# Masked graph attention on 8192 nodes: the first eight row blocks computed in four column quarters, with partial sums kept in DRAM

## The chip, the cores and the metric

One of the cores of a Trainium2 chip runs the kernel. The metric is the device time of one execution in microseconds (us), as the median of several runs.

## What is computed

The reference, cut to its core (N = 8192, D = 256):

```python
h = jnp.maximum(_layernorm(x, axis=-1), 0.0)
h1 = h @ a[:D]; h2 = h @ a[D:]
e = jax.nn.leaky_relu(h1 + h2.T, negative_slope=0.01)
attention = jnp.where(adj > 0, e, NEG_BIG)
attention = jax.nn.softmax(attention, axis=1)
out = x + attention @ h
```

The 8192 x 8192 adjacency matrix is int32 (256 MB) and is read once. The exponential of a leaky ReLU is a maximum of two products: up to a factor that depends on the row alone and cancels in the softmax, the weight of row i and column j is max(r_i, g_j) * q_j * mask_ij. So r (one number for a row) and g and q (one each for a column) are made once, and q is multiplied into h.

## The kernel before

**Tiling.** The rows of adj are cut into 16 *blocks* of 512, the columns into 16 *chunks* of 512. A chunk is also 512 rows of h, which are four tiles of 128. The kernel goes block by block, and in each block through all chunks, two to a *step*: 16 x 8 = 128 steps. A step has four *pairs* k = 0 to 3, a pair being two tiles of h (256 columns of adj).

**One pair** goes through the engines so: SyncE loads a 1 MB piece of adj (one for a chunk) into adj_in; ScalarE turns it into a byte mask (convert); TensorE transposes the mask into PSUM (transpose_mask, tile T); VectorE makes W = max(r_rep, g) * T (weights, two instructions of 512); ScalarE rounds W to w_hi (round_w); VectorE makes the rest, w_lo = W - w_hi (subtract), two pairs later in its own order; TensorE does 24 matmuls (products): for each of four row tiles t and two tiles of h, w_hi with h_hi, w_hi with h_lo, w_lo with h_hi, into acc, four PSUM banks. h_hi has two more columns that sum the weights. w_lo has two buffers: subtract of pair g waits until TensorE has used pair g - 2.

**The end of a block.** ScalarE copies the four banks of acc to SBUF as soon as each is done (evacuate), in the first step of the next block; VectorE makes the reciprocals of the sums (denominators), ScalarE scales (normalise), GpSimd adds x (finish), ScalarE issues the store. The row of r for the next block is laid out over all partitions by TensorE (lay_out_r) and ScalarE (copy_r) into r_rep.

**The first block** also makes h, a chunk at a time, while it uses it: stats (VectorE, LayerNorm statistics), norm (GpSimd, the reciprocal root), h_rows (ScalarE, normalise and ReLU), scores (VectorE, two dot products with a for each of four tiles: eight instructions of 256), exps (ScalarE: r, g, q), round_h (ScalarE) and rest_h (GpSimd, scaled h and its rest h_lo), and TensorE sums h for rows without neighbours (sum_h).

Every engine runs its own instructions in the order in which the code issues them, the same function `iteration` for each; order between engines is by semaphores alone. The kernel's last block ends with 20 small VectorE instructions and four stores.

## Time and profile before

| | |
|---|---|
| median of 3 runs | 1688.58 us (1687.75 to 1688.63) |
| profiled execution, its own time | 1690.27 us |
| its span in the profile | 1688.5 us |
| TensorE, VectorE, ScalarE, GpSimd busy | 97%, 85%, 69%, 13% of the span |
| TensorE's mean granted clock | 0.993 of full |
| DMA | 294 MB, 174 GB/s |

Busy shares are averages over the whole span. What bounds a stage is read from that stage: how long it takes, and for whom its engines wait there. Matmuls are pipelined, so each lasts longer (280 ns) than the distance between two.

### The profile page before, as it was taken

How to read it: one execution, taken by the hardware profiler on the slowest of the kernel's cores; microseconds unless marked ns; L12 is line 12 of the kernel's file. 1: busy time of each engine (PE TensorE's matmuls, PEld its weight loads, DVE VectorE, ACT ScalarE, POOL GpSimd, SP SyncE). 2: the span in 40 equal slices, each digit the busy share in tenths (PEclk: the TensorE clock that was granted, in tenths of full speed). 3: DMA queues.
4: the chain of work that ended last, by engine and by line, in shares of the span. 5: the costliest groups of instructions: out<-in, count | busy, mean ns of one | idle time of the engine just before them, and what ended most of it. 6: DMA issues, size and time to landing. Idle time of an engine off the chain costs nothing.

```text
span 1688.5 us, 40886 instructions
## 1 busy us (share of the span) xinstructions
PE 1630.9 (97%) x13504; PEld 1621.2 (96%) x13504; DVE 1440.1 (85%) x2008; ACT 1164.5 (69%) x1158; POOL 220.4 (13%) x309
## 2 busy tenths in 40 slices
PE   4887999999999999999999999999999999999998
PEld 3777999999999999999999999999999999999998
DVE  6999888888888888888888888888888888888887
ACT  5777766767676666767677676766767676676764
POOL 4667301001010100101010010101001010100100
PEclk9999999999999999999999999999999999999999
DMA  6443455555555555555555555555555455555552
GB/s 199 146 147 112 164 173 182 191 166 185 171 198 174 165 191 167 197 174 187 175 172 186 174 199 168 180 174 185 187 173 184 167 196 174 172 192 167 192 173 88
DMA packets 142672, 294.08 MB, mean 174 GB/s; under 512 B 4928, under 2 KB 5440, under 8 KB 142656
## 3 DMA queue, kind: packets, MB, share of 16 engines
q1 hardware_dynamic: 138336, 278.15, 49.4%
q10 hardware_dynamic: 4320, 15.73, 2.5%
q8 instruction: 8, 0.13, 0.0%
q14 instruction: 8, 0.07, 0.0%
HBM read 285.47 MB, written 8.39 MB: 174 GB/s over the span
## 4 chain that ended last, share of the span: by engine, by line
PE 89%; DVE 8%; issue 2%; DMA 1%; DVEq 0%; ACT 0%; POOL 0%; SPq 0%; ACTq 0%
PE acc L609 28%; PE acc L612 27%; PE acc L611 27%; PE T L567 6%; DVE rep L460 3%; DVE w_lo L481 2%; DVE W L471 1%; DVE bst L442 1%; PE rep L582 0%; DMA r_rep<-in_L_gnn_a_dram 0%; DVE mv L447 0%; DMA xb<-in_x_dram 0%; ACT hb L307 0%; DVE adj_in L552 0%; DVE adj_in L547 0%
## 5 line engine op out<-in xcount | busy, mean ns | idle before, releaser
L609 PE MATMUL acc<-h_hi,w_hi 128*128 (+1 forms) x4096 | 1186.2, 290 | 28.9 <-DVE w_lo L481 28.9
L612 PE MATMUL acc<-h_hi,w_lo 128*128 (+1 forms) x4096 | 1159.2, 283 | 0.0
L611 PE MATMUL acc<-h_lo,w_hi 128*128 (+1 forms) x4096 | 1153.8, 282 | 0.0
L350 ACT ACTIVATE w_hi<-W 128x1024 fp32r<-128x1024 f32 x512 | 540.5, 1059 | 420.3 <-DVE W L471 367.0
L609 PEld LDWEIGHTS acc<-h_hi,w_hi 128*128 128x128 f32 x4096 | 776.3, 190 | 33.5 <-issue 33.1
L471 DVE SCALAR_TENSOR_TENSOR W<-r_rep,g_all,T 128x512 f32<-128x512 int8 (+1 forms) x1024 | 720.1, 745 | 103.3 <-DVE w_lo L481 90.5
L611 PEld LDWEIGHTS acc<-h_lo,w_hi 128*128 128x128 f32 x4096 | 781.1, 191 | 0.2
L612 PEld LDWEIGHTS acc<-h_hi,w_lo 128*128 128x128 f32 x4096 | 777.4, 190 | 0.0
L481 DVE SCALAR_TENSOR_TENSOR w_lo<-W,w_hi 128x1024 fp32r<-128x1024 f32 x512 | 627.7, 1226 | 123.4 <-PE acc L612 109.4
L341 ACT ACTIVATE mask<-adj_in,mhalf 128x2048 fp8e5<-128x2048 int32 x256 | 509.2, 1989 | 24.7 <-issue 23.2
L271 POOL TENSOR_TENSOR xb<-xb,stage 128x256 f32<-128x256 f32 x60 | 41.3, 689 | 1381.6 <-ACT hb L379 1361.3
L567 PE MATMUL T<-ident,mask 128*128 128x128 f32 x1024 | 154.7, 274 | 4.1 <-ACT mask L341 4.1
L567 PEld LDWEIGHTS T<-ident,mask 128*128 128x128 f32 x1024 | 119.4, 141 | 5.1 <-ACT mask L341 5.1
L273 POOL TENSOR_TENSOR xb<-xb,hb 128x256 f32<-128x256 f32 x60 | 58.6, 976 | 4.7
L250 POOL TENSOR_TENSOR h_lo<-hq,h_hi 128x1024 f32 (+1 forms) x16 | 45.8, 2861 | 6.7 <-POOL hq L244 4.3
L369 ACT ACTIVATE stage<-acc 128x258 f32<-128x258 f32 x60 | 23.3, 388 | 16.5 <-PE acc L612 16.4
L307 ACT ACTIVATE hb<-xb,shift,rstd 128x256 f32<-128x256 f32 x32 | 16.6, 590 | 25.5 <-POOL shift L233 21.7
L378 ACT ACTIVATE stage<-stage,rinv 128x256 f32<-128x256 f32 x60 | 29.7, 496 | 0.0
L379 ACT ACTIVATE hb<-hb,zrow 128x256 f32<-128x256 f32 x60 | 29.7, 495 | 0.0
L460 DVE SCALAR_TENSOR_TENSOR rep<-stage,r_rep 128x256 f32<-128x256 f32 x64 | 29.5, 530 | 0.0
L460 DVE SCALAR_TENSOR_TENSOR rep<-hb,r_rep 128x256 f32<-128x256 f32 x56 | 26.0, 533 | 0.0
L307 ACT ACTIVATE stage<-xo,shift,rstd 128x256 f32<-128x256 f32 x32 | 16.6, 590 | 12.7 <-POOL shift L233 12.7
(58 smaller groups left out, 277.5 us busy)
## 6 DMA issues: line engine op xcount, KB each, us to landing
adj_in<-in_adj_dram SPq DMA_DIRECT2D x256, 1024.0 KB, 5.2
xb<-in_x_dram ACTq DMA_DIRECT2D x15, 512.0 KB, 3.2
out_dram<-xb ACTq DMA_DIRECT2D x15, 512.0 KB, 2.6
xb<-in_x_dram SPq DMA_DIRECT2D x8, 512.0 KB, 3.3
xo<-in_x_dram SPq DMA_DIRECT2D x8, 512.0 KB, 3.3
adj_in<-in_x_dram SPq DMA_DIRECT2D x1, 512.0 KB, 3.2
out_dram<-adj_in SPq DMA_DIRECT2D x4, 128.0 KB, 1.9
r_rep<-in_L_gnn_a_dram SPq DMA_DIRECT2D x1, 256.0 KB, 6.0
```

The costliest lines, as they stand in the source:

```text
L250: nc.gpsimd.tensor_tensor(h_lo[:, tiles, 0:D], hq[:, :, :], h_hi[:, tiles, 0:D].bitcast(f32), ALU.subtract)
L271: nc.gpsimd.tensor_tensor(xb[:, t, :], xb[:, t, :], stage[:, t, 0:D], ALU.add).then_inc(s_fin, 1)
L273: nc.gpsimd.tensor_tensor(xb[:, t, :], xb[:, t, :], hshare, ALU.add).then_inc(s_o, 1)
L341: nc.scalar.activation(mask8[:, kc, :, :].rearrange("p t j -> p (t j)"), adj_in[:, kc, :, :].rearrange("p t j -> p (t j)"), ACT.Sign, bias ...
L350: nc.scalar.activation(w_hi[:, k % HL, :], W[:, k % 2, :], ACT.Relu).then_inc(s_hi, 1)
L460: nc.vector.scalar_tensor_tensor(out[:, j, :], h[:, e, :], 1.0, a_rep[:, j * D:(j + 1) * D], ALU.mult, ALU.mult, accum_out=h12[:, parity, ...
L471: last = nc.vector.scalar_tensor_tensor(W[:, k % 2, u * BLK:(u + 1) * BLK], r_rep[:, b % 2, :], g_all[:, ds(G * c + e, 1)], T8[:, k // 2, ...
L481: nc.vector.scalar_tensor_tensor(w_lo[:, k % LL, :], W[:, k % 2, :], 0.0, w_hi[:, k % HL, :].bitcast(f32), ALU.max, ALU.subtract).then_inc ...
L567: last = nc.tensor.transpose(T[:, kc, t * P:(t + 1) * P], mask_words[:, kc, t, :], ident[:])
L609: nc.tensor.matmul(acc[:, t, 0:WC], w_hi[:, k % HL, cols], rhs_hi, start=start and u == 0, stop=False)
L611: nc.tensor.matmul(acc[:, t, 0:D], w_hi[:, k % HL, cols], rhs_lo, start=False, stop=False)
L612: last = nc.tensor.matmul(acc[:, t, 0:WC], w_lo[:, k % LL, cols], rhs_hi, start=False, stop=stop and u == 1)
```

## The change

Steps are no longer numbered by block. They are grouped in *visits* of a block, described by a tuple V. Blocks 0 to 7 are visited four times, each time for a quarter of the columns (4 chunks, 2 steps); blocks 8 to 15 once, for all 16 chunks (8 steps). The order: the first quarter of blocks 0 to 7 (visits 0 to 7), the second (8 to 15), the third (16 to 23), and then in turn the last quarter of block m and the whole of block m + 8 (visits 24 to 39). There are 32 short visits and 8 long ones, again 128 steps.

Between its quarters, the sums of a block lie in DRAM (part_sums). Chunks 0 to 3 of h are made in visit 0, chunks 4 to 7 in visits 1 to 4 (phase "whole"), and chunks 8 to 15 over two visits each, 5 and 6 to 19 and 20 (phases "early" and "late"); their rounding (made=) comes in the visit after.

```diff
+                if V.full:
+                    steps(V, V.n0, 0, True, False)
+                    with eng.Fori(1, WIDE - 1) as it:
+                        steps(V, V.n0 + it, it * CI, False, False)
+                    steps(V, V.n0 + WIDE - 1, NB - CI, False, True)
+                else:
+                    steps(V, V.n0, V.c0, True, False)
+                    steps(V, V.n0 + 1, V.c0 + CI, False, True)
...
+            def quarter(v, q, prev, make=None, phase=None, made=None, nxt=None, head=False, turn=False):
+                visit(Visit(v=v, n0=2 * v, b=v - SH * q, c0=Q * q, full=False, prev=prev,
+                            pb=SH - 1 if turn else v - 1 - SH * q, f=None,
+                            pa=v - SH - 1, make=make, phase=phase, made=made,
+                            nxt=v + 1 - SH * q if nxt is None else nxt,
+                            head=head, tail=False))
+            def finals(m, prev):
+                n0 = 2 * NPART + (2 + WIDE) * m
+                visit(Visit(v=NPART + 2 * m, n0=n0, b=m, c0=NB - Q, full=False, prev=prev, pb=m + SH - 1, f=2 * m - 1,
+                            pa=2 * SH - 1, make=None, phase=None, made=None, nxt=m + SH,
+                            head=False, tail=False))
+                tail = isinstance(m, int) and m == SH - 1
+                visit(Visit(v=NPART + 2 * m + 1, n0=n0 + 2, b=m + SH, c0=0, full=True, prev="rest", pb=m, f=2 * m,
+                            pa=2 * SH + m, make=None, phase=None, made=None, nxt=None if tail else m + 1,
+                            head=False, tail=tail))
+            def two(j, q1, q2, prev1, prev2, nxt=None):
+                quarter(5 + 2 * j, q1, prev1, make=SH + j, phase="early", made=SH - 1 + j, nxt=nxt)
+                quarter(6 + 2 * j, q2, prev2, make=SH + j, phase="late", turn=q2 != q1)
+            quarter(0, 0, None, head=True)
+            quarter(1, 0, "first", make=Q, phase="whole")
+            with eng.Fori(2, 5) as v:
+                quarter(v, 0, "first", make=v + 3, phase="whole", made=v + 2)
+            two(0, 0, 0, "first", "first")
+            two(1, 0, 1, "first", "first", nxt=0)
+            with eng.Fori(2, 5) as j:
+                two(j, 1, 1, "added", "added")
+            two(5, 1, 2, "added", "added", nxt=0)
+            with eng.Fori(6, 8) as j:
+                two(j, 2, 2, "added", "added")
+            quarter(21, 2, "added", made=NB - 1)
+            if h_made is not None:
+                h_made()
+            quarter(22, 2, "added")
+            quarter(23, 2, "added", nxt=0)
+            if h_summed is not None:
+                h_summed()
+            finals(0, "added")
+            with eng.Fori(1, SH - 1) as m:
+                finals(m, "full")
+            finals(SH - 1, "full")
```

SyncE: x of a later chunk (load_more_x) and the row of r, which is now stored to DRAM and read back over all partitions (load_r), stand among the loads of adj. A partition now holds rows p, p + 128, p + 256, p + 384 of a block of adj and x, where it held rows 4p to 4p + 3 (`adj.rearrange("(b t p) j -> b p t j")` in place of `"(b p t) j"`).

```diff
-            def load_adj(b, it, kc, wait):
-                n = b * NI + it
+            def load_more_x(c):
+                sp.wait_ge(s_z, G * c)
+                sp.sem_inc(s_lgate, 1)
+                sp.dma_start(x_bufs[0], x_w[c]).then_inc(s_x[0], 16)
+            def load_adj(b, c, n, kc, wait):
                 if wait:
                     sp.wait_ge(s_mask, n * CI + kc - 1)
-                sp.dma_start(adj_in[:, kc, :, :], adj_v[b, :, :, ds((it * CI + kc) * BLK, BLK)]).then_inc(
...
+            def load_r(V):
+                if V.head:
+                    sp.wait_ge(s_aps, 1)
+                    sp.wait_ge(s_dot, 2 * G * Q + 2)
+                    sp.wait_ge(s_rd, 16 * 2)
+                else:
+                    sp.wait_ge(s_rd, 16 * (V.nxt + 1))
+                    sp.sem_inc(s_lgate, 1)
+                    sp.wait_ge(s_w, PI * V.n0)
+                    sp.sem_inc(s_lgate, 1)
+                    sp.wait_ge(s_rr, 16 * V.v)
+                sp.sem_inc(s_lgate, 1)
+                sp.dma_start(r_rep[:, (V.v + 1) % 2, :], r_dram[ds(V.nxt, 1), :].partition_broadcast(P)).then_inc(
+                    s_rr, 16)
+            def steps(V, n, c, first, last):
+                if V.head and first:
                     load_x(0, 0, False)
-                    sp.dma_start(a_rep, a_row.partition_broadcast(P)).then_inc(s_a, 16)
+                    sp.dma_start(r_rep[:, 1, :], a_row.partition_broadcast(P)).then_inc(s_a, 16)
                     load_x(1, 1, False)
                 for kc in range(CI):
-                    if first_block and not first:
-                        load_x(it * CI + kc, kc, True)
-                    load_adj(b, it, kc, not (first_block and first))
-                if last and first_block:
-                    sp.wait_ge(s_z, NB)
-                    sp.sem_inc(s_stored, 16)
-            run(sp, iteration)
+                    if V.head and not first:
+                        load_x(c + kc, kc, True)
+                    load_adj(V.b, c + kc, n, kc, not (V.head and first))
+                    if V.phase in ("early", "whole") and first and kc == 0:
+                        load_more_x(V.make)
+                    if V.nxt is not None and last and kc == (1 if V.head else 0):
+                        load_r(V)
```

GpSimd: from chunk 4 on it sums h itself (sum_rows), and adds the earlier quarters to a block's sums (add_prior).

```diff
+            def sum_rows(c):
+                for e in range(G):
+                    pool.wait_ge(s_hs, G * (c - Q) + e + 1)
+                    nc.gpsimd.tensor_tensor(hsum[:], hsum[:], hb[:, e, :], ALU.add).then_inc(s_hs, 1)
+            def rest_h(c, parity):
                 pool.wait_ge(s_hh, c + 1)
                 pool.wait_ge(s_hq, c + 1)
                 tiles = ds(G * c, G)
@@ -253,86 +345,105 @@
                                         q4[:, parity, :].rearrange("p (e o) -> p e o", o=1),
                                         h_hi[:, tiles, D:D + 1].bitcast(f32), ALU.subtract).then_inc(s_hl, 1)
...
-            def finish(b, t):
-                i = G * b + t
+            def add_prior(V):
+                pool.wait_ge(s_prior, 16 * (V.pa + 1))
+                pool.wait_ge(s_free, G * V.v)
+                nc.gpsimd.tensor_tensor(stage[:, :, :], stage[:, :, :], prior, ALU.add).then_inc(s_add, 1)
...
+                if V.head:
+                    for kc in range(CI):
+                        if c + kc + 2 < Q:
+                            norm(c + kc + 2, kc)
+                        if c + kc + 1 < Q:
+                            scale_h(c + kc + 1, (kc + 1) % CI)
+                            rest_h(c + kc + 1, (kc + 1) % CI)
+                if V.made is not None and first:
+                    scale_h(V.made, 0)
+                    sum_rows(V.made)
+                if V.prev in ("added", "rest") and first:
+                    add_prior(V)
+                if V.phase in ("early", "whole") and first:
+                    norm(V.make, 0)
+                if V.made is not None and first:
+                    rest_h(V.made, 0)
+                if V.prev in ("full", "rest") and last:
+                    for t in range(G):
+                        finish(V.f, t)
+            run(pool, steps)
```

ScalarE: the new stores and loads are issued from its queue, and the work on h is spread over the pairs k = 0 to 7 of a short visit.

```diff
+            def store_r(c):
+                act.wait_ge(s_ex, c + 1)
+                if not isinstance(c, int) or c > 0:
+                    act.wait_ge(s_rd, 16 * c)
+                act.dma_start(r_cols[c], r_all[:, ds(G * c, G)]).then_inc(s_rd, 16)
...
+            def evacuate(V):
+                if V.prev in ("first", "added"):
+                    if isinstance(V.v, int) and V.v == 1:
+                        act.wait_ge(s_hl, Q)
+                        act.wait_ge(s_hsum, Q)
+                    else:
+                        act.wait_ge(s_part, 16 * (V.v - 1))
+                elif isinstance(V.f, int) and V.f == 0:
+                    act.wait_ge(s_part, 16 * NPART)
+                else:
+                    act.wait_ge(s_o, G * V.f)
+                for t in range(G):
                     if t < G - 1:
-                        act.wait_ge(s_acc, (G - 1) * b + t + 1)
+                        act.wait_ge(s_acc, (G - 1) * (V.v - 1) + t + 1)
                     else:
-                        act.wait_ge(s_used, (b + 1) * PB)
-                    if t == 0:
-                        if not isinstance(b, int) or b > 0:
-                            act.wait_ge(s_o, G * b)
...
+            def store_part(V):
+                if V.prev == "first":
+                    act.wait_ge(s_free, G * V.v)
+                    act.dma_start(part[V.pb], stage[:, :, :]).then_inc(s_part, 16)
+                else:
+                    act.wait_ge(s_add, V.pa + 1)
+                    act.dma_start(part[V.pb], stage[:, :, :]).then_inc(s_part, 16)
+            def load_prior(V):
+                if isinstance(V.pa, int) and V.pa == 0:
+                    act.wait_ge(s_z, G * Q)
+                else:
+                    act.wait_ge(s_add, V.pa)
+                act.wait_ge(s_part, 16 * (V.pa + 1))
+                act.dma_start(prior, part[V.pb]).then_inc(s_prior, 16)
...
+            def side_work(V, k):
+                if V.made is not None:
+                    if k == 0:
+                        round_h(V.made, 0, [0, 1])
+                    if k == 2:
+                        round_h(V.made, 0, [2, 3])
+                        store_r(V.made)
+                if V.prev is not None:
+                    if k == 1:
+                        evacuate(V)
+                if V.phase == "whole":
+                    if k == 3:
+                        h_rows(V.make, 0, [0, 1])
+                    if k == 4:
+                        h_rows(V.make, 0, [2, 3])
+                if V.phase == "early":
+                    if k == 6:
+                        h_rows(V.make, 0, [0, 1])
+                    if k == 7:
+                        h_rows(V.make, 0, [2, 3])
+                if V.phase in ("whole", "late") and k == 7:
+                    exps(V.make, 0)
+                if V.prev in ("first", "added") and k == 4:
+                    store_part(V)
+                if V.prev in ("added", "rest") and k == 0:
+                    load_prior(V)
+                if V.prev in ("full", "rest"):
+                    if k == 2:
+                        load_x_again(V)
+                    if k == 4:
+                        normalise(V.f, 0)
+                    if k == 5:
+                        normalise(V.f, 1)
+                    if k == 6:
+                        normalise(V.f, 2)
+                        normalise(V.f, 3)
+                    if k == 7:
+                        store_out(V)
```

VectorE: scores now read a from PSUM (a_ps); statistics and scores are spread over the pairs of a visit.

```diff
+                    dve.wait_ge(s_z, G * c + e + 1)
                     for j in range(2):
                         dve.wait_ge(s_dot, 2 * G * c + 2 * e + j + 1)
-                        nc.vector.scalar_tensor_tensor(out[:, j, :], h[:, e, :], 1.0, a_rep[:, j * D:(j + 1) * D],
+                        nc.vector.scalar_tensor_tensor(out[j], h[:, e, :], 1.0, a_ps[:, j * D:(j + 1) * D],
                                                        ALU.mult, ALU.mult, accum_out=h12[:, parity, j, e:e + 1]
                                                        ).then_inc(s_dot, 1)
...
+            def side_work(V, k):
+                if V.phase == "whole":
+                    if k == 1:
+                        stats(V.make, 0, V.make - 1, [0, 1])
+                    if k == 2:
+                        stats(V.make, 0, V.make - 1, [2, 3])
+                    if k >= 4:
+                        scores(V.make, 0, [k - 4])
+                if V.phase == "early" and 1 <= k <= 4:
+                    stats(V.make, 0, V.make - 1, [k - 1])
+                if V.phase == "late" and k >= 4:
+                    if k == 4 and V.prev == "added":
+                        dve.wait_ge(s_add, V.pa + 1)
+                    scores(V.make, 0, [k - 4])
+                if V.prev in ("full", "rest") and k == 4:
+                    denominators(V)
```

**VectorE, where h is made.** Before, in the first block, all of a chunk's work on h (the statistics in tile mv, the eight scores in rep) stands between the weights of two pairs:

```order
L442 BN_STATS bst<-xo 128x6 x4
L447 BN_AGGR mv<-bst 128x2 x4
L481 SCALAR_TENSOR_TENSOR w_lo<-W,w_hi 128x1024
L471 SCALAR_TENSOR_TENSOR W<-r_rep,g_all,T 128x512 x2
L460 SCALAR_TENSOR_TENSOR rep,h<-hb,r_rep 128x256 x8
L481 SCALAR_TENSOR_TENSOR w_lo<-W,w_hi 128x1024
```

In the changed kernel, in visit 1 from its third pair on (the first half of the statistics stands just ahead), the same work is in pieces, one piece to a pair:

```order
L659 SCALAR_TENSOR_TENSOR w_lo<-W,w_hi 128x1024
L614 BN_STATS bst<-xb 128x6 x2
L620 BN_AGGR mv<-bst 128x2 x4
L649 SCALAR_TENSOR_TENSOR W<-r_rep,g_all,T 128x512 x2
L659 SCALAR_TENSOR_TENSOR w_lo<-W,w_hi 128x1024
L649 SCALAR_TENSOR_TENSOR W<-r_rep,g_all,T 128x512 x2
L659 SCALAR_TENSOR_TENSOR w_lo<-W,w_hi 128x1024
L638 SCALAR_TENSOR_TENSOR xo,h<-hb,a_ps 128x256 x2
L649 SCALAR_TENSOR_TENSOR W<-r_rep,g_all,T 128x512 x2
```

A pair of weights and its subtract now have at most a quarter of a chunk's scores or half its statistics beside them.

**GpSimd, the same chunks.** Before, in the loop over the first block's steps, it does the norm of one chunk and the scaled h (hq) and rest of the next:

```order
L226 TENSOR_TENSOR rstd<-mv,eps 128x4
L229 TENSOR_TENSOR nmean<-zeros,mv 128x4
L231 TENSOR_TENSOR rstd<-rstd,mhalf 128x4
L233 TENSOR_TENSOR shift<-nmean,rstd 128x4
L244 TENSOR_SCALAR hq<-stage,q 128x256 x4
L250 TENSOR_TENSOR h_lo<-hq,h_hi 128x1024
L252 TENSOR_TENSOR h_hi<-q,h_hi 128x4
```

Now, in visit 21 (the last one that finishes a chunk) and the four after it, hsum and the earlier sums (xo) are added as well; the visits 9, 11, ... 19 have the norm too, between the sum into stage and h_lo:

```order
L327 TENSOR_SCALAR hq<-hb,q 128x256 x4
L335 TENSOR_TENSOR hsum<-hsum,hb 128x256 x4
L352 TENSOR_TENSOR stage<-stage,xo 128x1032
L342 TENSOR_TENSOR h_lo<-hq,h_hi 128x1024
L344 TENSOR_TENSOR h_hi<-q,h_hi 128x4
L352 TENSOR_TENSOR stage<-stage,xo 128x1032 x4
```

Four instructions of 256 and one of 1032 elements a partition stand between the exponentials and the rest of h (h_lo).

**SyncE, the start.** Now, in visit 0 and the first step of visit 1, the row of r (r_rows) stands ahead of the fifth piece of adj:

```order
L231 DMA xb<-in_x_dram 128x1024
L243 DMA adj_in<-in_adj_dram 128x4x512
L231 DMA xo<-in_x_dram 128x4x256
L243 DMA adj_in<-in_adj_dram 128x4x512
L258 DMA r_rep<-r_rows 128x512
L243 DMA adj_in<-in_adj_dram 128x4x512
L237 DMA xb<-in_x_dram 128x1024
```

Before, the fifth piece followed the load of x alone, with no load of r anywhere in the queue.

## Rows read from the trace of the kernel before

**Rows 1.** Busy time by stretch: stretch, length, engines (instructions), granted clock, DMA, GB/s.

```profile
32.10:195.30 163.20, 133.88 (x933) 126.68 (x932) 152.63 (x416) 125.57 (x220) 105.97 (x142) 0.94 0.42 140
195.30:1681.30 1486.00, 1486.00 (x12539) 1486.00 (x12538) 1263.97 (x1502) 1022.32 (x909) 101.61 (x133) 1.00 0.53 178
1681.30:1688.50 7.20, 0.32 (x3) 0.12 (x1) 4.50 (x19) 0.00 (x0) 0.00 (x0) 0.76 0.21 73
```

**Rows 2.** The same view, one block of the steady part.

```profile
294.10:393.20 99.10, 99.10 (x839) 99.10 (x838) 84.49 (x101) 68.60 (x61) 6.79 (x9) 1.00 0.54 180
```

**Rows 3.** Waits, whole span: who waited for whom, us in total, times, longest.

```profile
PE acc L609 <- DVE w_lo L481: 28.9, 14, 2.8
```

**Rows 4.** Timeline of VectorE, one chunk of the first block: start, duration.

```profile
71.62 1.41 DVE L471 SCALAR_TENSOR_TENSOR W<-r_rep,g_all,T 128x512 f32<-128x512 f32 x2 [0.22 <-DVE w_lo L481]
72.94 1.40 DVE L442 BATCH_NORM_STATS2 bst<-xo 128x6 f32<-128x256 f32 x4
...
74.80 1.20 DVE L481 SCALAR_TENSOR_TENSOR w_lo<-W,w_hi 128x1024 fp32r<-128x1024 f32 x1
76.24 1.41 DVE L471 SCALAR_TENSOR_TENSOR W<-r_rep,g_all,T 128x512 f32<-128x512 f32 x2 [0.24 <-DVE w_lo L481]
77.56 0.79 DVE L460 SCALAR_TENSOR_TENSOR rep<-hb,r_rep 128x256 f32<-128x256 f32 x1
...
80.94 1.22 DVE L481 SCALAR_TENSOR_TENSOR w_lo<-W,w_hi 128x1024 fp32r<-128x1024 f32 x1
82.38 0.75 DVE L471 SCALAR_TENSOR_TENSOR W<-r_rep,g_all,T 128x512 f32<-128x512 f32 x1 [0.22 <-DVE w_lo L481]
```

**Rows 5.** Timeline of VectorE, three instructions that wait for nobody.

```profile
189.42 1.40 DVE L471 SCALAR_TENSOR_TENSOR W<-r_rep,g_all,T 128x512 f32<-128x512 int8 x2 [0.28 <-DVE w_lo L481]
190.74 1.22 DVE L481 SCALAR_TENSOR_TENSOR w_lo<-W,w_hi 128x1024 fp32r<-128x1024 f32 x1
192.06 1.41 DVE L471 SCALAR_TENSOR_TENSOR W<-r_rep,g_all,T 128x512 f32<-128x512 int8 x2
```

**Rows 6.** Timeline of GpSimd: two rests of h, one scaled h, one sum of 256.

```profile
33.10 2.22 POOL L250 TENSOR_TENSOR h_lo<-hq,h_hi 128x1024 fp32r<-128x1024 f32 x1
72.93 1.84 POOL L244 TENSOR_SCALAR hq<-stage,q 128x256 f32<-128x256 f32 x4 [3.00 <-ACT q L321]
75.11 2.94 POOL L250 TENSOR_TENSOR h_lo<-hq,h_hi 128x1024 f32 x1 [0.34 <-POOL hq L244]
576.07 0.64 POOL L271 TENSOR_TENSOR xb<-xb,stage 128x256 f32<-128x256 f32 x1 [75.55 <-ACT hb L379]
```

**Rows 7.** Timeline of VectorE beside the first row of rows 6.

```profile
33.16 2.45 DVE L460 SCALAR_TENSOR_TENSOR rep<-hb,r_rep 128x256 f32<-128x256 f32 x1
35.53 0.46 DVE L460 SCALAR_TENSOR_TENSOR rep<-hb,r_rep 128x256 f32<-128x256 f32 x1
```

**Rows 8.** Timeline of ScalarE at a block's end: first and last of four evacuations.

```profile
590.94 0.39 ACT L369 ACTIVATE stage<-acc 128x258 f32<-128x258 f32 x1 [0.21 <-PE acc L612]
...
593.00 0.39 ACT L369 ACTIVATE stage<-acc 128x258 f32<-128x258 f32 x1 [0.33 <-PE acc L612]
```

**Rows 9.** DMA issues of the page: count, KB each, median us to landing.

```profile
adj_in<-in_adj_dram SPq DMA_DIRECT2D x256, 1024.0 KB, 5.2
xb<-in_x_dram ACTq DMA_DIRECT2D x15, 512.0 KB, 3.2
```

**Rows 10.** Landing time of the first piece of adj alone, issued at 2.1 us.

```profile
DMA to landing us min/median/max: 9.1/9.1/9.1
```

**Rows 11.** Timelines at the start: ScalarE's first mask, VectorE's first weights, TensorE's first product.

```profile
17.52 1.99 ACT L341 ACTIVATE mask<-adj_in,mhalf 128x2048 fp8e5<-128x2048 int32 x1
21.86 1.38 DVE L471 SCALAR_TENSOR_TENSOR W<-r_rep,g_all,T 128x512 f32<-128x512 f32 x2
32.12 0.47 PE L609 MATMUL acc<-h_hi,w_hi 128*128 128x258 f32 x1
```

**Rows 12.** Group by line: GpSimd's reciprocal root, count, us busy, mean ns.

```profile
L231 POOL TENSOR_TENSOR rstd<-rstd,mhalf 128x4 f32<-128x4 f32 x16 | 19.5, 1217 | 0.0
```

## What I predicted before the run

> **What bounds the kernel now.** I first cut the span into stretches [rows 1]. From 195.3 to 1681.3 us TensorE is busy without a gap at full clock, while VectorE works 85% of the time: this part is TensorE's. A block takes 99.10 us there [rows 2], in about 836 matmuls, four of which lay out r; without them it is 98.6, or **12.33 us for a step** and 3.08 for a pair. From 32.1 to 195.3 us VectorE is busy 152.6 of 163.2 us and TensorE 82%, at a granted clock of 0.94: this stretch is VectorE's. It does the first block, 8 steps, for which TensorE would need 98.6. In the whole trace TensorE waits for w_lo at only 14 places, 28.9 us in all [rows 3]; the rest of its loss lies in stretched work and in the order of its queue. After the last product 7.2 us follow, which the change leaves alone.
>
> So the floor with VectorE out of the way is a start, 128 x 12.33, and 7.2. Before, the first product begins at 32.12 [rows 11], and 32.1 + 1578.2 + 7.2 = 1617.5; 15 blocks lose another 7 to the lay-outs, and the first block 64. These two sum to the span of 1688.5 and are all that the change can win, except for an earlier start. What VectorE does to a chunk is in [rows 4]: from the weights at 71.62 to those at 82.38 pass 10.76 us, of which 1.86 are statistics (72.94 to 74.80) and 3.38 scores (77.56 to 80.94), the rest two pairs. A pair that waits for nobody takes 2.64 us [rows 5], up to 2.76 with the write that the weights wait for [rows 4]; I take **2.7**. Against 3.08, VectorE has 0.38 us to spare in a pair and 3.1 in a short visit. Making one chunk costs it about 5.
>
> **The start, visit 0.** I followed the new order from semaphore to semaphore with the durations of [rows 4], [rows 6] and [rows 11]. ScalarE now converts the first mask ahead of h_rows; its data land at 2.1 + 9.1 = 11.2 us [rows 10], so h_rows starts at 13.2 where it could have at 11.6. But scores now follow tile by tile, and end at 17 as before. The mask was 1.99 us between exps and the copy of r [rows 11]; that is gone, and VectorE's first weights start at 19.9 in place of 21.86. The subtract stands right behind, and TensorE starts at about 27 in place of 32.1. From there on each chunk is a chain: ScalarE h_rows, exps, round_h and two roundings, GpSimd norm and rest, VectorE the rest. I get weights of pairs 2, 4 and 6 at 31.4, 42.6 and 52.9 us, no faster than the 10.76 of [rows 4]. Then SyncE: the load of r stands ahead of the fifth piece of adj and waits for the last scores (51.5). So that piece lands at about 57.7 (5.2 to 5.8 after its issue, [rows 9]), while ScalarE stands in its convert since 54.5 and, behind that, roundings of pairs 6 and 7; TensorE waits with pair 5 behind the transposes. A one-time stall of 3 us. **TensorE begins visit 1 at 71 us.** 126 steps remain: 71 + 1553 + 7 = **1631**. Bounds: 65 with the stall hidden, 75 with every wait a little longer.
>
> **Visits 1 to 4**, a whole chunk each. VectorE needs 8 x 2.7 + 1.9 + 3.1 = 26.6 against 24.7: +2 for visit 1. In visits 2 to 4 a wait is added: h_rows of the next chunk, at k = 3 on ScalarE, waits for the rest of the chunk before (s_hl), whose GpSimd work now stands behind four additions of 256 and the norm. By rows: scaled h 1.84 [rows 6], additions 4 x 0.64 to 0.9, norm some 2.3 with its root of 1.2 [rows 12], but h_lo can't start before round_h at k = 2, about 11 us after the exps; with its 2.2 to 2.9 [rows 6] s_hl comes at 14. Behind h_rows on ScalarE stands the convert of k = 4, and VectorE's scores wait for the tile. From exps to exps: 14 + 0.6 + 12.5 (four pairs with scores) + 1.9 = 29 against 24.7, so **+4.5 three times, 13.5** (from 2 each, with the wait hidden, to 6).
>
> **Visits 5 to 20**, half a chunk each. Statistics: 21.6 + 1.9 = 23.5; scores: 21.6 + 3.1 = 24.7. By themselves both fit. What doesn't is GpSimd. At 33.10 it starts h_lo, and VectorE's score of 33.16 lasts 2.45 in place of 0.46, until GpSimd is done at 35.3 [rows 6, 7]. At 75.11 it is the other way round: h_lo lasts 2.94, because VectorE's subtract runs until 76.0 [rows 4, 6]. So instructions with two SBUF inputs keep each other out; weights read T from PSUM and ran on beside it. The subtract is such an instruction, and so are h_lo, the 0.64 us sums [rows 6] and the new add_prior of 1032 elements, which I price as h_lo, 2.2. If it begins during a subtract it runs on for 2.2 us over weights of 1.3 and delays the next subtract by 0.8; if it begins during weights, by up to 2.2. I take 1.15 for each long one, 0.1 for a short one, 0.3 for the norm. Visits 9 to 20 are six couples: early 23.5 + 2 x 1.15 + 0.4 + 0.3 = 26.5 (+1.8), late 24.7 + 1.15 = 25.8 (+1.1), **6 x 2.9 = 17**. Visits 5 to 8 have no add_prior: +1. Bounds: 0, as VectorE has slack in other pairs and is one or two pairs ahead, to 2.2 for each long one, 35.
> The Trainium skill (SBUF — State Buffer, "SBUF: two separate sides") says that the pair of ports that VectorE and GpSimd share is an exclusive lock, held for the whole instruction, and that the second one blocks fully. By that rule read as 2.2 us for every long instruction the term would be 35; the one row with VectorE second shows it (2.45), the others only 0.3 (0.79 at 77.56).
>
> **Ends of visits.** 39 in place of 15. At a block's end ScalarE spends 2.5 us on evacuation, since it follows TensorE bank by bank (590.94 to 593.4 [rows 8]), and yet blocks take 99.10 without a gap. The stores and loads of sums (0.5 MB, priced as x, 3.2 us to landing [rows 9]) have from k = 4 to the next k = 1. DMA was at 0.53 of its time [rows 1] and gains a quarter in short visits: hidden. The row of r comes a step early: hidden. ScalarE works 8.5 us a step [rows 2], 17 in a short visit, plus 4 for h, 2.5 and up to three issues: near 24.7, no more. Denominators and finish lie in slack as before. For all this and for half-clock stretches while TensorE isn't full, 3 (0 to 20). Removed lay-outs are in the 12.33.
>
> **Sum.** 1631 + 2 + 13.5 + 1 + 17 + 3 = 1667.5, a span 21 shorter. The profiled run's own time was 1.8 over its span and 1.7 over the median; the difference of spans applied to the median, 1688.6 - 21, gives **1668 us**.
>
> **Rivals.**
> *VectorE and GpSimd don't hurt each other* in visits 5 to 20 (for: scores now read PSUM, and only 0.3 us was lost per chunk before): 1667.5 - 17 - 3 = 1648. Chance 0.2.
> *Ends of visits cost TensorE*, the other side: ScalarE's evacuation stands ahead of the convert and of round_w of k = 2, and behind it now come round_h, h_rows and DMA issues. If of each of the 24 new ends 1.2 us is exposed, it takes 29 and the kernel is slower, at 1697; it decides from 0.75 each (18 us). All 2.5 exposed would give 1728. For: ScalarE near 24 of 24.7. Against: none of 15 ends shows a gap. 0.15.
> *Adj comes slower.* Consecutive 2 KB pieces of a partition now lie 128 rows x 32 KB = 4 MB apart, before 32 KB. If that doubled the 5.2 us of a piece [rows 9], two would take 20.8 against 12.33 a step, some 2670 us; up to 6 us a piece it is hidden. No row shows such a stride, and the 512 rows read are the same. 0.02.
> The Trainium skill (DMA: Bandwidth & Descriptors, "Latency and other measured facts") reports half the rate for a row pitch of 4 MiB from partition to partition; that pitch here shrinks.
> *The quarters win nothing*: visit 0's chain and the waits of visits 1 to 4 repeat through visit 20, 4.5 each: 1631 + 90 - 30 for what overlaps, near 1688. 0.08.
> The forecast has 0.55, its own range 1658 to 1680.
>
> **Range and chances.** 1647 to 1690 takes in the first rival, the forecast and the last; outside are some 0.15 to 0.2. A change within 0.2%, 3.4 us, can't be told from none here. Faster 0.78 (0.55, 0.2, a little of the last), within 0.06, slower 0.16.
>
> **What would show it.** TensorE's first product at 27 us and visit 1's at 71; ScalarE waiting for the fifth adj piece; visits 2 to 4 at 29 us; couples 9 to 20 at 52 in place of 49.3; subtracts of over 1.3 us beside GpSimd's long additions; full blocks at 98.6. Wrong would make it: couples at 49.3 (first rival), or TensorE waiting at ends of visits 21 to 24, where no h is made (second).

## The result: 1671.3 us, 1.0% faster, and the profile after

The changed kernel takes **1671.31 us** (median of 4 runs, 1669.16 to 1673.48) against 1688.61 of the kernel before beside it: ratio 0.9897, 95% interval 0.9882 to 0.9913. I had forecast 1668, so the direction and the size hold. The terms of my sum do not all hold. Two of them are wrong and cancel, and that is luck.

The page of the changed kernel, its first lines and two groups:

```profile
span 1668.8 us, 39111 instructions
...
PE 1604.5 (96%) x13350; PEld 1594.2 (96%) x13350; DVE 1439.5 (86%) x2008; ACT 1184.9 (71%) x1240; POOL 359.2 (22%) x367
...
L659 DVE SCALAR_TENSOR_TENSOR w_lo<-W,w_hi 128x1024 fp32r<-128x1024 f32 x512 | 657.5, 1284 | 136.4 <-ACT w_hi L461 65.0
...
L352 POOL TENSOR_TENSOR stage<-stage,xo 128x1032 f32<-128x1032 f32 x24 | 75.6, 3148 | 212.7 <-ACT stage L480 212.6
```

GpSimd's addition of prior sums (L352) takes 3.15 us on the mean, while the subtraction (L659) that my forecast had it hold up is hardly longer than one alone, 1.28 against 1.22. In the waits, whole span, these three are of interest beside [rows 3]:

```profile
ACT stage L515 <- POOL xb L362: 40.3, 22, 2.7
PE T L769 <- ACT mask L452: 37.5, 13, 13.3
...
PE acc L807 <- DVE w_lo L659: 4.7, 4, 1.4
```

TensorE's 28.9 us of waits for w_lo are down to 4.7. It waits 37.5 us for masks from ScalarE, 25.5 of them before 60 us, at the start. Behind 770 us its transposes wait 14 times for 1.0 to 1.9 us, 22.3 us in all; the profile puts part of these down to the masks and part to VectorE's W. ScalarE in turn waits 40.3 us for GpSimd (L515 is the division of a finished tile, L362 GpSimd's last addition to a tile). By stretch, in the columns of [rows 1], these are the start to visit 1, visit 1, visits 2 to 4, 5 to 25, 26 to the last product, and the tail:

```profile
25.60:70.60 45.00, 33.30 (x225) 32.14 (x225) 30.77 (x78) 28.42 (x48) 15.95 (x22) 0.85 0.44 134
70.60:96.50 25.90, 25.49 (x209) 24.83 (x208) 24.45 (x48) 20.29 (x27) 7.79 (x11) 1.00 0.64 200
96.50:180.30 83.80, 78.33 (x626) 75.05 (x626) 79.64 (x146) 64.01 (x86) 36.54 (x43) 1.00 0.62 199
180.30:773.80 593.50, 592.51 (x4995) 592.24 (x4994) 540.82 (x771) 447.21 (x480) 163.91 (x141) 1.00 0.72 220
773.80:1661.60 887.80, 866.48 (x7272) 863.80 (x7271) 746.42 (x896) 611.42 (x581) 123.42 (x119) 1.00 0.61 186
1661.60:1668.80 7.20, 0.50 (x5) 0.29 (x3) 4.66 (x19) 0.00 (x0) 0.00 (x0) 0.88 0.22 73
```

In 180.3 to 773.8 us, where I had put 17 us of loss, TensorE stands still for 1 us. From 773.8 us on, where the final visits are, it stands still for 21.3 us.

For a finer account I took the start of TensorE's first product of each visit from the trace and subtracted 12.33 us for each of its steps. What is left is the visit's loss:

| part | forecast | measured |
|---|---|---|
| first product starts | 27 | 25.6 |
| visit 1 starts | 71 | 70.6 |
| loss of visit 1 | 2 | 1.3 |
| of visits 2 to 4 | 13.5 | 9.7 (3.3, 3.3, 3.2) |
| of visits 5 to 8 | 1 | 0 |
| of visits 9 to 20 | 17 | 0.1 |
| of visits 21 to 38 (ends and clock) | 3 | 27.5 (0.4 before visit 25) |

From visit 26 on each quarter loses 2.0 us and each whole visit some 1.7; one whole visit, 27, loses 3.6. The quarters lose it in one pair, k = 6, which takes 5.2 us.

**How a final visit loses 2 us.** ScalarE at the end of visit 26 (start, duration), after the third tile, which it normalises from 788.83 us on:

```profile
791.97 0.51 ACT L515 ACTIVATE stage<-stage,rinv 128x256 f32<-128x256 f32 x1 [2.25 <-POOL xb L362]
792.39 0.49 ACT L516 ACTIVATE hb<-hb,zrow 128x256 f32<-128x256 f32 x1
792.79 1.04 ACT L461 ACTIVATE w_hi<-W 128x1024 fp32r<-128x1024 f32 x1
794.45 0.41 ACTq L521 DMA_DIRECT2D out_dram<-xb  x1
795.00 2.00 ACT L452 ACTIVATE mask<-adj_in,mhalf 128x2048 fp8e5<-128x2048 int32 x1 [1.18 <-POOL xb L362]
```

And GpSimd beside it, the third tile and the fourth:

```profile
789.80 1.32 POOL L360 TENSOR_TENSOR xb<-xb,stage 128x256 f32<-128x256 f32 x1 [1.33 <-ACT hb L516]
791.19 0.74 POOL L362 TENSOR_TENSOR xb<-xb,hb 128x256 f32<-128x256 f32 x1
792.96 0.64 POOL L360 TENSOR_TENSOR xb<-xb,stage 128x256 f32<-128x256 f32 x1 [1.02 <-ACT hb L516]
793.67 0.74 POOL L362 TENSOR_TENSOR xb<-xb,hb 128x256 f32<-128x256 f32 x1
```

One buffer, hshare, carries a tile's part of the mean row to GpSimd. Tiles 2 and 3 are both normalised at k = 6, so the second waits 2.25 us for GpSimd to be done with the first. The rounding of k = 7 stands behind that wait. The store of the block, which waits for the fourth tile (to 794.4), comes next, and behind it the mask, from 795.0 to 797.0. TensorE's transposes of this mask are the wait that costs the time:

```profile
797.14 0.65 PE L769 MATMUL T<-ident,mask 128*128 128x128 f32 x4 [1.74 <-DVE W L649]
```

The profile names VectorE's W here, which ends at 797.0 too. By the code the transposes need only the weights of k = 7, done at 792.0, and in e1 and e2 below they start 0.13 us behind the end of the mask, as here. So it is the mask.

In the kernel before the four tiles were spread: one in the first step of a block, one each at k = 0, 1 and 2 of the last, and the store after k = 3. Its block of 8 steps lost 0.5 us in all [rows 2], the lay-outs of r included.

### The profile page after: what moved, and what is told of

It is laid out like the page before. It is cut to its first block, busy times and chain, and to the rows that moved or that the text cites. A ratio compares the mean times of both kernels' runs of the same rounds, so it can differ in the third digit from the quotient of the medians.

```text
span 1668.8 us, 39111 instructions
## 1 busy us (share of the span) xinstructions
PE 1604.5 (96%) x13350; PEld 1594.2 (96%) x13350; DVE 1439.5 (86%) x2008; ACT 1184.9 (71%) x1240; POOL 359.2 (22%) x367
## 4 chain that ended last, share of the span: by engine, by line
PE 76%; ACT 6%; issue 5%; POOL 4%; DVE 3%; ACTq 1%; DVEq 0%; POOLq 0%
PE acc L807 24%; PE acc L810 23%; PE acc L809 23%; PE T L769 6%; ACT mask L452 2%; POOL xb L362 2%; ACT w_hi L461 2%; POOL xb L360 1%; ACT hb L516 1%; DVE W L649 1%; DVE w_lo L659 1%; ACT stage L515 1%; POOL h_hi L344 0%; ACTq L521 0%; ACTq L506 0%
## 5 line engine op out<-in xcount | busy, mean ns | idle before, releaser
L807 PE MATMUL acc<-h_hi,w_hi 128*128 128x258 f32 (+1 forms) x4096 | 1185.2, 289 | 5.9 <-DVE w_lo L659 4.7
L810 PE MATMUL acc<-h_hi,w_lo 128*128 128x258 f32 (+1 forms) x4096 | 1156.9, 282 | 0.0
L809 PE MATMUL acc<-h_lo,w_hi 128*128 128x256 f32 (+1 forms) x4096 | 1151.8, 281 | 0.0
L649 DVE SCALAR_TENSOR_TENSOR W<-r_rep,g_all,T 128x512 f32<-128x512 f32 (+1 forms) x1024 | 718.3, 743 | 70.9 <-DVE w_lo L659 45.7
L659 DVE SCALAR_TENSOR_TENSOR w_lo<-W,w_hi 128x1024 fp32r<-128x1024 f32 x512 | 657.5, 1284 | 136.4 <-ACT w_hi L461 65.0
L769 PE MATMUL T<-ident,mask 128*128 128x128 f32 x1024 | 156.0, 275 | 48.3 <-ACT mask L452 37.5
L352 POOL TENSOR_TENSOR stage<-stage,xo 128x1032 f32<-128x1032 f32 x24 | 75.6, 3148 | 212.7 <-ACT stage L480 212.6
L327 POOL TENSOR_SCALAR hq<-hb,q 128x256 f32<-128x256 f32 x56 | 37.7, 691 | 217.7 <-ACT q L424 217.7
L480 ACT ACTIVATE stage<-acc 128x258 f32<-128x258 f32 x156 | 58.2, 383 | 32.3 <-PE acc L810 30.6
L362 POOL TENSOR_TENSOR xb<-xb,hb 128x256 f32<-128x256 f32 x60 | 62.7, 1044 | 4.7
L515 ACT ACTIVATE stage<-stage,rinv 128x256 f32<-128x256 f32 x60 | 30.0, 500 | 40.3 <-POOL xb L362 40.3
L335 POOL TENSOR_TENSOR hsum<-hsum,hb 128x256 f32<-128x256 f32 x48 | 46.9, 978 | 2.8
L638 DVE SCALAR_TENSOR_TENSOR xo<-hb,a_ps 128x256 f32<-128x256 f32 x96 | 36.2, 412 | 3.6 <-ACT hb L408 2.7
L342 POOL TENSOR_TENSOR h_lo<-hq,h_hi 128x1024 fp32r<-128x1024 f32 (+1 forms) x16 | 35.6, 2224 | 6.1 <-ACT h_hi L443 5.6
```

Of the source, the lines that this page charges most:

```text
L352: nc.gpsimd.tensor_tensor(stage[:, :, :], stage[:, :, :], prior, ALU.add).then_inc(s_add, 1)
L362: nc.gpsimd.tensor_tensor(xb[:, t, :], xb[:, t, :], hshare, ALU.add).then_inc(s_o, 1)
L480: nc.scalar.activation(stage[:, t, :], acc[:, t, 0:WC], ACT.Copy).then_inc(s_free, 1)
L649: last = nc.vector.scalar_tensor_tensor(W[:, k % 2, u * BLK:(u + 1) * BLK], r_rep[:, V.v % 2, :], g_all[:, ds(G * c + e, 1)], T8[:, k // 2 ...
L659: nc.vector.scalar_tensor_tensor(w_lo[:, k % LL, :], W[:, k % 2, :], 0.0, w_hi[:, k % HL, :].bitcast(f32), ALU.max, ALU.subtract).then_inc ...
L769: last = nc.tensor.transpose(T[:, kc, t * P:(t + 1) * P], mask_words[:, kc, t, :], ident[:])
```

## Experiments

Every ratio below is to the kernel before on the same chip. The losses are worked out as above. "Half clock" counts the stretches of 3.41 us (two of 6.83) in which TensorE was granted 1.2 GHz instead of 2.4, in visits 5 to 38. Losses and stretches are those of one profiled execution, and executions of one kernel differ: the changed kernel's four had a mean clock of 0.991 to 0.994 of full (the profiled one 0.994), and e4's profiled one, at 1672.67 us, was its slowest (the fastest took 1666.60).

| kernel | median us, ratio (95%) | visit 1 starts | loss 2-4 | 5-23 | 24-38 | half clock |
|---|---|---|---|---|---|---|
| changed | 1671.31, 0.9897 (0.9882-0.9913) | 70.6 | 9.7 | 0.5 | 27.1 | 1 |
| e1 two shares | 1648.92, 0.9765 (0.9752-0.9777) | 70.2 | 9.7 | 0.5 | 6.2 | 0 |
| e2 store later | 1648.30, 0.9759 (0.9747-0.9772) | 69.7 | 9.7 | 0.5 | 5.7 | 0 |
| e4 rows early | 1670.05, 0.9883 (0.9868-0.9897) | 70.1 | 6.8 | 0.5 | 32.6 | 3 |
| e5 adj first | 1666.32, 0.9866 (0.9852-0.9881) | 64.7 | 9.7 | 0.5 | 29.3 | 2 |
| e6 more GpSimd | 1694.29, 1.0035 (1.0021-1.0048) | 70.2 | 9.7 | 24.3 | 33.1 | 8 |
| e7 more scores | 1700.39, 1.0065 (1.0052-1.0078) | 69.1 | 9.7 | 17.4 | 42.2 | 8 |
| e8 both | 1719.82, 1.0187 (1.0174-1.0200) | 70.3 | 9.7 | 40.9 | 36.1 | 9 |
| e9 all repairs | 1634.07, 0.9675 (0.9663-0.9688) | 64.3 | 5.2 | 0.5 | 0.2 | 0 |
| f1 = e9 + GpSimd behind | 1640.77, 0.9713 (0.9700-0.9726) | 65.0 | 6.8 | 7.3 | 0.2 | 0 |
| f2 = e9 + scores | 1651.68, 0.9778 (0.9764-0.9791) | 64.3 | 6.8 | 17.9 | 0.2 | 0 |
| f3 = e9, narrow rest | 1630.55, 0.9654 (0.9641-0.9667) | 64.2 | 3.2 | 0.5 | 0.2 | 0 |
| f4 = f1 + scores | 1656.79, 0.9811 (0.9797-0.9824) | 63.8 | 6.9 | 22.9 | 0.2 | 0 |

### The ends of visits: e1 and e2

e1 gives the share a second buffer:

```
-        hmean, hshare = hb[:, 0, :], hb[:, 1, :]
+        hmean, hshare = hb[:, 0, :], [hb[:, 1, :], hb[:, 2, :]]
...
-                if not isinstance(f, int) or i > 0:
-                    act.wait_ge(s_o, i)
+                if not isinstance(f, int) or i > 1:
+                    act.wait_ge(s_o, i - 1)
...
-                nc.scalar.activation(hshare, hmean, ACT.Copy, scale=zrow[:, t:t + 1]).then_inc(s_y, 1)
+                nc.scalar.activation(hshare[t % 2], hmean, ACT.Copy, scale=zrow[:, t:t + 1]).then_inc(s_y, 1)
```

> The sixteen final visits lose some 27 us in the changed kernel: the pair k=6 of each quarter takes 5.2 us in place of 3.2, and the whole ones lose some 1.7 us each. Theory A: ScalarE's rounding of the next pair stands in its program order behind L515, which waits for GpSimd's finish of the tile before (L362), because one buffer holds the share of the mean row. With two of these buffers taken in turn, and the wait set one tile further back, it need not wait: the loss falls by the 7 x 2.0 us of the quarters and about as much in the whole visits, to a time of about 1646 us (1642 to 1652). Rival B: ScalarE simply has too much to do in these pairs (evacuations, masks, four normalisations), whatever it waits for: then the time stays within 5 us of 1671. My prediction on record, in which the ends cost 3 us in all, leaves nothing to win: 1668 to 1671.

It took 22.4 us off. e2 leaves the buffer alone and issues the store of a block at k = 0 of the next visit:

```
-                act.wait_ge(s_o, G * (V.f + 1))
-                act.dma_start(out_t[V.pb], xb[:, :, :]).then_inc(s_out, 16)
+                act.wait_ge(s_o, G * V.f)
...
-                    if k == 7:
+                    if k == 0 and not (isinstance(V.f, int) and V.f == 0):
                         store_out(V)
```

> The store of a finished block of output, which ScalarE issues at k=7 after waiting for GpSimd's last finish (L362), is issued at k=0 of the next visit instead. Theory A: ScalarE's wait before the store also stands ahead of a rounding, but while the waits of L515 remain ahead of it, only the last of them is saved: 2 to 10 us less, 1661 to 1669. Rival B: the rounding of k=7 stands before it already and the store's wait is covered: 1671. A cost is possible too: the store is then later, and the load of x into the same buffer, two pairs on, waits for it: some 16 x 1 us more, 1687.

It took 23.0 off, much more than I expected. ScalarE in e2, at the same place of visit 26:

```profile
789.87 0.51 ACT L515 ACTIVATE stage<-stage,rinv 128x256 f32<-128x256 f32 x1 [2.24 <-POOL xb L362]
...
790.68 1.05 ACT L461 ACTIVATE w_hi<-W 128x1024 fp32r<-128x1024 f32 x1
791.63 1.99 ACT L452 ACTIVATE mask<-adj_in,mhalf 128x2048 fp8e5<-128x2048 int32 x1
```

And in e1:

```profile
787.48 0.49 ACT L515 ACTIVATE stage<-stage,rinv 128x256 f32<-128x256 f32 x1
...
792.06 2.00 ACT L452 ACTIVATE mask<-adj_in,mhalf 128x2048 fp8e5<-128x2048 int32 x1 [2.73 <-POOL xb L362]
```

In e2 the wait of 2.24 us is still there and hardly costs anything, since the mask follows the rounding at once. In e1 that wait is gone, and the store's wait ahead of the mask has grown to 2.73 us, but it starts from an earlier time. Counted from the start of the visit (773.80 in the changed kernel, 771.72 in e2, 772.44 in e1) the mask comes at 21.2, 19.9 and 19.6 us, so 1.3 and 1.6 earlier; by just these amounts the visit's loss falls, from 2.0 to 0.7 and 0.45. So it is not one wait that costs the 2 us but two in a row on ScalarE, in front of the mask for which TensorE's transposes wait; without either the rest is nearly covered. Each kernel still loses 5.7 to 6.2 us there. With both edits (e9) the loss is 0.2. That ScalarE's amount of work is the cause (rival B of e1) is refuted: the work is the same.

### The one-time stall: e5

```
                     load_adj(V.b, c + kc, n, kc, not (V.head and first))
+                    if isinstance(V.v, int) and V.v == 1 and first and kc == 0:
+                        load_r(V._replace(head=True, v=0, nxt=1))
...
-                    if V.nxt is not None and last and kc == (1 if V.head else 0):
+                    if V.nxt is not None and last and kc == 0 and not V.head:
```

> Once, in visit 0, a pair takes 11.1 us in place of some 4, behind a ScalarE mask (L452) that waits 5.7 us for its piece of the adjacency matrix. Theory A: that piece is late since its issue on SP's queue stands behind the load of r for visit 1, which itself waits for r to be stored. Here the load of r is issued behind that piece, everything else unchanged: the pair falls to about 5.5 us, time about 1666 us. Rival B: the piece is late because the transfers compete in this stretch, or r then comes late and the same time is lost at the start of visit 1: then 1671, or more.

In the changed kernel ScalarE stands in this row, in visit 0, and TensorE behind it:

```profile
57.23 2.00 ACT L452 ACTIVATE mask<-adj_in,mhalf 128x2048 fp8e5<-128x2048 int32 x1 [5.69 <-DMA adj_in<-in_adj_dram]
```

In e5 the same mask starts at 52.05 us without a wait, and visit 1 at 64.7 instead of 70.6. The mechanism is as I had described it; I had priced it at 3 us and it costs 5.9. The whole kernel gains 5.0; in the profiled execution 2.2 us more are lost in the final visits, with a second half-clock stretch.

### Visits 2 to 4: e4 and f3

e4 lets h_rows start when GpSimd has added the first row tile of its buffer, in place of waiting for the rest of h:

```
-                        act.wait_ge(s_hl, c)
+                        if isinstance(c, int) and c <= Q:
+                            act.wait_ge(s_hl, c)
+                        else:
+                            act.wait_ge(s_hs, G * (c - Q) + 1)
```

> In visits 2, 3 and 4 a TensorE visit is 3.2 to 3.3 us longer than its two plain steps. Theory A: ScalarE's rows of h (L408) for the second chunk made in a visit stand behind the wait for the rest of the first chunk of h (L344), which GpSimd has late because its scaling comes after other work; behind them waits the rounding of weights. Here these rows wait only until GpSimd has added the rows of the buffer that they overwrite (L335), not for the rest: 2 of the 3.2 us go in each of the three visits, 6 us in all, time about 1665 us. Rival B: these visits are long because VectorE is full in them (26.5 us of 27.9 busy): then the time stays within 2 us of 1671. My prediction on record put 4.5 us on each of the three visits for the same wait, and would give 1661.

The wait of the changed kernel, ScalarE in visit 2, is this one:

```profile
104.59 1.10 ACT L408 ACTIVATE hb<-xb,shift,rstd 128x256 f32<-128x256 f32 x2 [2.07 <-POOL h_hi L344]
```

In e4 the same instruction starts at 101.99 without one. Yet each visit gains only 1.0 us (9.7 to 6.8 for the three): pair k = 2 falls from 4.1 to 3.3, pair k = 1 stays at 4.5. The whole kernel gains 1.3, which its interval does not tell from nothing. The trace shows where the rest went: it has three half-clock stretches in the final visits where the changed kernel has one, and loses 5.5 more there, in visits that the edit does not touch.

What holds pair k = 1? In the changed kernel GpSimd, and below it VectorE:

```profile
101.13 2.21 POOL L342 TENSOR_TENSOR h_lo<-hq,h_hi 128x1024 f32 x1 [1.17 <-ACT h_hi L443]
```

```profile
101.34 3.09 DVE L659 SCALAR_TENSOR_TENSOR w_lo<-W,w_hi 128x1024 fp32r<-128x1024 f32 x1
```

f3 computes that rest of h for 8 of its 256 columns in the chunks finished in visits 2 to 4, the other columns being zero; it builds on e9, which has all four repairs:

```
-                nc.gpsimd.tensor_tensor(h_lo[:, tiles, 0:D], hq[:, :, :], h_hi[:, tiles, 0:D].bitcast(f32),
+                nc.gpsimd.tensor_tensor(h_lo[:, tiles, 0:w], hq[:, :, 0:w], h_hi[:, tiles, 0:w].bitcast(f32),
```

> The version with all four repairs, in which the rest of h (L342 of the changed kernel) of the chunks made in visits 1 to 4, those of which it is finished in a visit of phase whole, is computed for 8 of 256 columns; the others are set to zero once by VectorE in the head. Visits 3 and 4 still lose 2.2 us each and visit 2 0.8, with a pair k=1 of 4.5 us, in which this subtraction of GpSimd (3.12 us) meets the subtraction of w_lo on VectorE (3.09 in place of 1.22). Theory A: the lock between the two makes the loss: the pairs fall to 3.1, some 1.5 to 2 us less in each of visits 3 and 4, 3 to 5 us in all, 1630, less what the zeroing costs at the start (0 to 3 us). Theory B: the pair is long for ScalarE, whose h_hi comes just before it: these visits stay as they are, 1634 to 1637.

At that place of visit 3, GpSimd and VectorE of f3:

```profile
120.21 0.25 POOL L344 TENSOR_TENSOR h_lo<-hq,h_hi 128x32 f32 x1 [1.15 <-ACT h_hi L448]
```

```profile
120.42 1.22 DVE L667 SCALAR_TENSOR_TENSOR w_lo<-W,w_hi 128x1024 fp32r<-128x1024 f32 x1
```

Pair k = 1 falls from 4.5 to 2.9 us and the visit's loss from 2.3 to 1.1. The edit shortens GpSimd's own subtraction too, so I also looked for the meeting alone. The trace of e9 has it both ways round, with the same instructions. GpSimd and VectorE in visit 2, which loses 0.8 us, and in visit 3, which loses 2.3:

```profile
95.24 3.12 POOL L344 TENSOR_TENSOR h_lo<-hq,h_hi 128x1024 f32 x1 [1.53 <-ACT h_hi L448]
95.08 1.22 DVE L667 SCALAR_TENSOR_TENSOR w_lo<-W,w_hi 128x1024 fp32r<-128x1024 f32 x1
...
120.64 2.22 POOL L344 TENSOR_TENSOR h_lo<-hq,h_hi 128x1024 f32 x1 [1.17 <-ACT h_hi L448]
120.84 3.10 DVE L667 SCALAR_TENSOR_TENSOR w_lo<-W,w_hi 128x1024 fp32r<-128x1024 f32 x1
```

Where VectorE starts first, pair k = 1 takes 2.9 us, and where GpSimd does, 4.5. So of the 3.25 us of each of these visits 1.0 is the wait for the rest of h, 1.2 to 1.5 the meeting of GpSimd's and VectorE's subtractions, and the rest is not taken apart. The whole kernel gains 3.5 us over e9.

### VectorE's room and GpSimd: e6, e7, e8, then f1, f2, f4

e6 put two GpSimd additions ahead of the prior's in the late visits; e7 computes the scores of the late visits twice; e8 does both. The added results are not read. The additions stand inside add_prior, which visits 6 and 8 don't call, so the trace has them in six visits, not in the eight that the expectations name: 12 additions, which at 1.15 us each would be 14 us and not 18.

```
                 pool.wait_ge(s_free, G * V.v)
+                if V.phase == "late":
+                    nc.gpsimd.tensor_tensor(hq[:, :, :], prior[:, :, 0:D], prior[:, :, 0:D], ALU.add)
+                    nc.gpsimd.tensor_tensor(h_lo[:, ds(NT - G, G), 0:D], prior[:, :, 0:D], prior[:, :, 0:D], ALU.add)
                 nc.gpsimd.tensor_tensor(stage[:, :, :], stage[:, :, :], prior, ALU.add).then_inc(s_add, 1)
```

> Visits 6, 8, ... 20 do two additional GpSimd additions of 1024 elements each, in front of the addition of the prior sums; their results go to places not read later, so only work is added. The theory of my prediction: each long GpSimd addition holds up one long subtraction of VectorE by 1.15 us, and VectorE has no room in these visits: 16 x 1.15 = 18 us more, about 1689. Rival theory, from the trace of the changed kernel, where visits 5 to 20 take 24.66 us for two steps of 12.33 and so lose nothing: VectorE has 3.4 us of room in 49.4, and it is GpSimd that waits when the two meet (3.12 us for an addition that takes 1.9 alone): 0 to 2 us more, 1671 to 1673.

> Visits 6, 8, ... 20 compute each of their eight scores a second time (a product with a running sum left out, 256 wide, result not used): some 8 x 0.34 = 2.7 us more of VectorE's time in each, 8 visits. The theory of my prediction, in which VectorE's time in these visits is already more than TensorE's: all of it shows, 8 x 2.7 = 22 us more, 1693. Rival theory: VectorE has 3.4 us of room in the 49.4 us of an early and a late visit, so 2.7 us more fit on the sum, though the late visit alone has less room than the couple: 0 to 8 us more, 1671 to 1679.

> Both additions together: two more GpSimd additions and eight more VectorE products in each of visits 6, 8, ... 20. If the two engines hold each other up only once VectorE has no room left (theory of the room), the sum is more than its parts: the 16 long GpSimd additions, free alone, now cost up to 1.15 us each, so 10 to 25 us over the run with the products alone. If holding up never costs VectorE anything here, it equals the run with the products alone within 3 us. If my prediction's prices are right at any load, it is 22 + 18 = 40 us over the changed kernel, 1711.

e6 is not the test that I meant it to be for a second reason. GpSimd's second extra and the prior's addition, then VectorE, in visit 10 of e6:

```profile
306.39 1.89 POOL L354 TENSOR_TENSOR h_lo<-xo 128x1024 fp32r<-128x1024 f32 x1
308.24 3.39 POOL L355 TENSOR_TENSOR stage<-stage,xo 128x1032 f32<-128x1032 f32 x1
```

```profile
306.72 2.63 DVE L662 SCALAR_TENSOR_TENSOR w_lo<-W,w_hi 128x1024 fp32r<-128x1024 f32 x1 [0.54 <-ACT w_hi L464]
311.86 0.42 DVE L641 SCALAR_TENSOR_TENSOR xo<-hb,a_ps 128x256 f32<-128x256 f32 x1 [2.50 <-POOL stage L355]
```

VectorE's scores wait 2.5 us until the prior sums are added, because the scores write into their buffer (xo). Ahead of that the subtraction, which started 0.33 us behind GpSimd, takes 2.63 us in place of 1.22. The 23 us that e6 lost hold both, and 6 us in the final visits besides, so its number speaks for neither theory. e8 costs 19.4 us over e7, inside the 10 to 25 of the theory of the room, but it has the same new wait and decides nothing either. In e7 the late visits lose 1.6 to 1.8 us and the early ones behind them 0.5. That fits VectorE's room in a late visit. VectorE is busy 22.29 of 24.68 us in an early visit of the changed kernel and 23.65 in a late one:

```profile
278.85:303.53 24.68, 24.68 (x210) 24.68 (x209) 22.29 (x30) 20.14 (x23) 9.20 (x8) 1.00 0.75 233
303.53:328.21 24.68, 24.68 (x211) 24.68 (x209) 23.65 (x42) 18.52 (x21) 9.28 (x9) 1.00 0.76 235
```

2.7 us more into 1.03 of room leaves 1.7. At 1700 us e7 is outside both ranges that I had given. My rival, which took the room over both visits together, is refuted. But 42.2 - 27.1 = 15.1 us of what e7 lost lie in final visits, which it does not change, under eight half-clock stretches. So three runs repeat the test on e9, where nothing waits at the ends. f1 places the two additions behind the prior's:

```
                     add_prior(V)
+                if V.phase == "late" and first:
+                    fixed = h_hi[:, 0:G, 0:D].bitcast(f32)
+                    pool.wait_ge(s_hl, V.make)
+                    nc.gpsimd.tensor_tensor(hq[:, :, :], fixed, fixed, ALU.add)
+                    nc.gpsimd.tensor_tensor(h_lo[:, ds(NT - G, G), 0:D], fixed, fixed, ALU.add).then_inc(s_spare, 1)
+                    pool.wait_ge(s_spare, V.make - (SH - 1))
```

> The version with all four repairs, 1634, in which visits 5 to 20 lose nothing and no half-clock stretch disturbs the sum, plus two more GpSimd additions of 1024 elements in each late visit (6, 8, ... 20), this time behind the addition of the prior sums, where nobody waits for them; their results are not read. The earlier run with such additions put them ahead of it, and VectorE's scores waited for it. Theory A, the lock: each addition meets one subtraction and holds it up by 1.2 to 1.4 us, and the late visit has 24.68 - 23.65 = 1.03 us of room on VectorE, so 2 x 1.3 - 1.0 = 1.6 us more in each of 8 visits, 13 us, 1647. Theory B, only GpSimd waits: 1634 to 1636.

> The version with all four repairs plus the doubled scores in the late visits (8 x 0.34 = 2.7 us of VectorE's time each, results not used). Theory A: on top of the changed kernel these cost 29 us, of which only 17 lay in the visits that had them and some 12 to 15 in later ones, unchanged, through half-clock stretches after waits of TensorE of 2 us; with those waits repaired only the 8 x (2.7 - 1.0) = 14 us, or up to 17 with the early visits behind them, are left: 1648 to 1651. Rival: doubled scores cost 29 us wherever they stand, 1663.

> The version with all four repairs plus both the doubled scores and the two GpSimd additions behind the prior's. The room of the late visits is used up by the scores, so each hold-up must show whole. Theory A, the lock: the run with scores alone plus 16 x 1.3 = 21 us, about 1670. Theory B, only GpSimd waits when the two meet: the run with scores alone, 1649, within 2 us.

f2 costs 17.6 us over e9; the visits with the scores and those behind them lose 17.4 of it in the traces. (f1, f2 and f4 also lose 1.5 us more than e9 in visit 2, where GpSimd's subtraction starts first.) f1 costs 6.7, between the theories, and its trace says why. GpSimd in visit 10 of f1, and then VectorE:

```profile
295.69 3.12 POOL L355 TENSOR_TENSOR stage<-stage,xo 128x1032 f32<-128x1032 f32 x1 [13.82 <-ACT stage L492]
298.76 2.89 POOL L388 TENSOR_TENSOR hq<-h_hi 128x1024 f32<-128x1024 f32 x1
301.61 1.89 POOL L389 TENSOR_TENSOR h_lo<-h_hi 128x1024 fp32r<-128x1024 f32 x1
```

```profile
295.31 1.23 DVE L674 SCALAR_TENSOR_TENSOR w_lo<-W,w_hi 128x1024 fp32r<-128x1024 f32 x1 [0.57 <-PE acc L825]
...
298.58 1.31 DVE L674 SCALAR_TENSOR_TENSOR w_lo<-W,w_hi 128x1024 fp32r<-128x1024 f32 x1 [0.54 <-ACT w_hi L473]
...
301.82 2.77 DVE L674 SCALAR_TENSOR_TENSOR w_lo<-W,w_hi 128x1024 fp32r<-128x1024 f32 x1
```

Three meetings. In the first two VectorE's subtraction starts first (295.31 and 298.58) and takes its usual time, and GpSimd's addition is the long one: 3.12 and 2.89 us. In the third GpSimd starts first, by 0.21 us, takes 1.89, and the subtraction takes 2.77 in place of 1.22. **Who starts second pays.** Of the 16 additions the four of visits 6 and 8, which have no prior sums, run in the visit before; subtractions of 1.69 and 1.41 us stand beside them there, and the visit loses nothing. Of the other twelve only every second one starts ahead of a subtraction. Per such visit VectorE pays 1.55 once, less 1.03 of room: 0.5 expected, 0.7 seen, with 0.5 in the visit behind. In f4 the room is gone, and the same meeting (a subtraction of 2.10 us) shows nearly whole: 2.71 in place of 1.80 us per late visit, 0.9 each, 5.1 over f2. That is neither the 21 us of theory A nor the nothing of theory B: six meetings count, not sixteen.
The Trainium skill (SBUF — State Buffer, "SBUF: two separate sides") has this rule: of such a pair of instructions whichever starts first keeps the shared ports for its whole length, and the other is blocked. These rows agree with it, both ways round.

### All four repairs: e9

> All four repairs at once: two buffers for the share, the output stored one visit later, the rows of h not waiting for the rest of the chunk before, the load of r behind the adjacency piece. They lie in different stretches, except the first two, so theory A says they add: 25 + 2 (beyond the first) + 6 + 5 = 38 us less than the changed kernel, 1634 (1628 to 1642). Rival B, by which the final visits lose to ScalarE's amount of work: 11 us less at most, 1660. With everything removed that steady steps do not need, the bound is 126 x 12.33 = 1553 plus the start of 71 less 5 and the tail of 7, 1627, and the two stores of the rest.

1634.07 us, 3.2% faster than the kernel before and 37 us less than the changed kernel. The parts add: 6.3 at the start, 4.5 in visits 2 to 4, 26.9 at the ends. Of the 4.5, 1.5 come from visit 2 alone, where VectorE's subtraction happened to start first; in f1, f2 and f4, which have the same code there, it did not, and these visits gain 2.9.

## Why the prediction came out right, and which steps of it did not hold

The number came out right because two wrong terms cancel; the mechanism was right for the start and for one of the two waits in visits 2 to 4, and wrong for visits 9 to 20 and for the ends.

- **The start and VectorE's stretch held.** "TensorE begins visit 1 at 71 us": 70.6. The stall behind the load of r was there, twice as long as my 3 us, and the chains of chunks around it that much shorter, since the sum of 71 held. Visits 21 to 24 and the tail are as forecast.
- **"A wait is added ... +4.5 three times, 13.5"** had the right wait and the wrong size: 9.7. Only 1.0 us of each 3.25 hangs on s_hl (e4). Another 1.2 is the meeting of the subtractions (f3), which I had not put into these visits.
- **"I take 1.15 for each long one ... 6 x 2.9 = 17" failed.** It measured 0.1, for two reasons. The first is the price of a meeting. I had read one row of each order and averaged over them. In fact add_prior is released by the evacuation, at the same point of every visit, some 0.4 us after a subtraction has begun (0.30 to 0.45 in the twelve visits), so GpSimd waits every time (3.1 to 3.4 us). I had put 0.8 us on this order too, taking the next subtraction to stand 1.4 us behind the last; it stands 2 us behind, since VectorE waits for ScalarE and TensorE in between, and is held up by 0.1 to 0.3. h_lo is of the other order in each early visit and does hold a subtraction up, by 0.65 us. In visit 9 h_lo and the subtraction behind it, and add_prior of visit 10:

```profile
287.05 2.20 POOL L342 TENSOR_TENSOR h_lo<-hq,h_hi 128x1024 f32 x1
288.46 1.87 DVE L659 SCALAR_TENSOR_TENSOR w_lo<-W,w_hi 128x1024 fp32r<-128x1024 f32 x1
...
304.19 3.12 POOL L352 TENSOR_TENSOR stage<-stage,xo 128x1032 f32<-128x1032 f32 x1 [13.80 <-ACT stage L480]
```

  The second is the room. My budget for VectorE was too dear: its 26.5 and 25.8 us for an early and a late visit measured 22.3 and 23.7 busy, hold-ups included (23.2 and 23.6 if only its waits for ScalarE and TensorE are taken off), so what it was held up by fitted into the 24.7. I had named couples at 49.3 us as the sign against this term, and they are at 49.4. My bound of 35 us was mis-added as well: 18 long ones at 2.2 come to 37 in the same sum.
- **"Denominators and finish lie in slack as before ... 3 (0 to 20)" failed.** Ends and clock took 27.5. I had checked that ScalarE's amount of work fits in 24.7 us (it measured 20.1 and 18.5 in an early and a late visit), and not the waits in its order. Two normalisations moved into one slot, and the store came to stand ahead of a mask.
- The two wrong terms are -17 and +24.5, the rest is -6; the span of 1668.8 is 1.3 us from my sum of 1667.5. The rivals at 1648 and 1697, which I had taken as alternatives, both came true in part at the same time: no time lost to VectorE and GpSimd in visits 9 to 20, though they do hold each other up, and ends that cost TensorE 27 us. For the second I had named evacuation; e1 and e2 show the waits for GpSimd and leave the evacuation as it was.
- **The stride** cost nothing: a piece of adj lands within a median of 5.4 us, before 5.2 [rows 9].

## What to carry to other kernels

When work is folded into fewer slots of an in-order engine, list the waits in the order of its queue, not only its busy time: two waits in a row in front of something that TensorE needs cost 27 us here, and removing either one won 22 of them back. For two engines that exclude each other, find out which of them starts first in each meeting, who waits for the other, and whether the one that waits has room; an average over starts gave 17 us where the kernel paid nothing. Compare small edits only on a version in which TensorE does not wait elsewhere, since what the clock takes behind such waits can be as much as they take themselves, and it differs from execution to execution.

## What the runs showed that I had not expected

Behind some of TensorE's waits its clock falls. Windows of the changed kernel, end of visit 27 (columns as in [rows 1], the granted clock third from the right):

```profile
893.00:897.00 4.00, 2.98 (x25) 2.77 (x23) 2.94 (x3) 2.04 (x2) 1.26 (x2) 1.00 0.44 145
897.00:899.10 2.10, 1.25 (x11) 1.25 (x12) 0.40 (x1) 2.10 (x3) 0.00 (x0) 1.00 0.03 8
899.10:902.50 3.40, 3.40 (x18) 3.40 (x18) 2.23 (x3) 1.56 (x4) 0.00 (x0) 0.50 0.97 288
```

At 0.50, 1.2 GHz, TensorE does 18 matmuls in 3.4 us where it otherwise does some 30. Visit 27 loses 3.6 us where its like lose 1.7, so a stretch costs some 2 us more, as much again as the wait. The wait ahead of this stretch, the one at the same place of visit 29, which no stretch follows, and that in e7, which one follows:

```profile
897.85 0.65 PE L769 MATMUL T<-ident,mask 128*128 128x128 f32 x4 [1.87 <-ACT mask L452]
...
1026.42 0.65 PE L769 MATMUL T<-ident,mask 128*128 128x128 f32 x4 [1.47 <-ACT mask L452]
```

```profile
1044.62 0.96 PE L772 MATMUL T<-ident,mask 128*128 128x128 f32 x4 [2.27 <-ACT mask L452]
```

The same instructions of visits 24 to 38 had 1 stretch in the changed kernel, 2 in e5, 3 in e4 and 8 in e7, whose edits lie hundreds of us earlier and leave these visits as they are. Whether the edits or the execution made the difference is not shown for 1, 2 and 3: the times of e4's four executions alone lie 6 us apart. This is how e4's own 3 us disappeared in its trace, and how half of e7's loss came about. In all versions that wait for nothing there (e9, f1 to f4) the count is 0. What decides whether a stretch follows a wait was not tried and remains open.
